# Other places in a block for a layer step's matmuls, its own-node product and two splits

## The reference

```python
x = _layernorm(x + _L0_gnn_ref(x, adj, W0, b0))     # D^-1/2 (A+I) D^-1/2 x W0^T + b0
x = _layernorm(x + _L1_gnn_ref(x, adj, WQ, WK, p))  # att[i,j] = p . relu(q[j] + k[i]), masked softmax over j, times x
x = _layernorm(x + _L2_gnn_ref(x, adj, W2, b2))     # as layer 0, with |A+I| in the degrees
x = _layernorm(x + _L3_gnn_ref(x, adj, W3, b3))     # without the identity added
```

## Time and profile before

| What | Value |
|---|---|
| median of 3 runs | 14251.69 us (14249.84 to 14259.41) |
| profiled execution, its own time | 14255.09 us |
| its span, first to last instruction | 14253.3 us |
| opening, to the first score matmul | 240.7 us |
| attention of the eight graphs | 240.7 to 14072.4 us |
| closing | 180.9 us |

### The profile page before, as it was taken

One profiled execution on the slowest core, in us unless ns is written; L12 is line 12 of the kernel. 1 busy time (PEld: TensorE's weight loads), 2 busy tenths in 40 slices (PEclk: granted clock), 3 DMA queues, 4 the chain that ended last, 5 costly groups with the idle time before them and its releaser, 6 DMA issues.

```text
span 14253.3 us, 317325 instructions
## 1 busy us (share of the span) xinstructions
PE 13023.6 (91%) x143877; PEld 5459.3 (38%) x143877; DVE 13509.2 (95%) x14168; ACT 13092.2 (92%) x8612; POOL 668.9 (5%) x495
## 2 busy tenths in 40 slices
PE   6889989999899988999989998899989999899988
PEld 3333334443344333443334433344333433333333
DVE  5999999999999999999999999999999999999995
ACT  5999899998999899998999989999899998998994
POOL 0000000000000000000000000000000000000000
PEclk7999999999999999999999999999999999999999
DMA  5111112221122111221122211222112221011103
GB/s 184 45 51 47 49 52 86 85 61 50 55 86 87 62 40 63 87 87 56 36 72 84 86 56 36 75 84 85 56 35 75 88 78 56 30 49 51 42 12 108
DMA packets 714328, 935.44 MB, mean 66 GB/s; under 512 B 61713, under 2 KB 455953, under 8 KB 693521
## 3 DMA queue, kind: packets, MB, share of 16 engines
q1 hardware_dynamic: 712976, 915.13, 20.5%
HBM read 722.01 MB, written 184.55 MB: 64 GB/s over the span
## 4 chain that ended last, share of the span: by engine, by line
PE 45%; DVE 35%; ACT 16%; issue 2%; DMA 2%; SPq 0%; POOL 0%; ACTq 0%; DVEq 0%; POOLq 0%
PE score L1134 33%; DVE big L990 31%; ACT big L756 14%; PE acc L1057 6%; PE turn L1034 2%; PE acc L1116 2%; DVE att L941 2%; DVE gx L871 1%; DMA piece<-adj_turned 1%; DMA big<-in_adj_dram 0%; ACT y_turned L679 0%; DVE stats L877 0%; ACT turned L669 0%; DMA q_pair_kept<-turned 0%; PE acc L1075 0%
## 5 line engine op out<-in xcount | busy, mean ns | idle before, releaser
L990 DVE TENSOR_SCALAR big<-q_pair,k_pair_cols 128x2048 f32<-128x2048 f32 x10240 | 12366.6, 1281 | 380.0 <-PE score L1134 362.6
L756 ACT ACTIVATE big<-q_f,k_cols 128x2048 f32<-128x2048 f32 x6144 | 11746.9, 1999 | 70.2 <-DMA q_f<-q_kept 44.1
L1134 PE MATMUL score<-big,unit_window 128*32 128x512 f16 x81920 | 5178.8, 396 | 819.0 <-DVE big L990 788.4
L1134 PE MATMUL score<-big,sign_window 128*32 128x512 f32 x49152 | 5619.7, 597 | 273.2 <-ACT big L756 268.6
L1134 PEld LDWEIGHTS score<-big,unit_window 128*32 128x32 bf16 x81920 | 2270.4, 96 | 4003.1 <-DVE big L990 1242.9
L1134 PEld LDWEIGHTS score<-big,sign_window 128*32 128x32 f32 x49152 | 1569.0, 110 | 3603.8 <-issue 3005.9
L1057 PE MATMUL acc<-piece,gs 128*128 128x512 f32 x3072 | 1446.6, 598 | 36.0 <-DMA piece<-adj_turned 23.6
L1057 PEld LDWEIGHTS acc<-piece,gs 128*128 128x128 f32 x3072 | 533.8, 191 | 545.4 <-issue 459.1
L737 ACT ACTIVATE att_turned<-turn 128x512 f32<-128x512 f32 x512 | 300.9, 588 | 390.5 <-PE turn L1034 389.7
L593 POOL TENSOR_SCALAR att_var<-att_mom 128x1 f32<-128x1 f32 x128 | 66.0, 515 | 10641.0 <-DVE att_mom L959 10641.0
L1116 PE MATMUL acc<-x,att_turned 128*128 128x128 f32 x4096 | 554.9, 279 | 0.0
(11 more groups left out here) (88 smaller groups left out, 2592.0 us busy)
## 6 DMA issues: line engine op xcount, KB each, us to landing
piece<-adj_turned SPq DMA_DIRECT2D x1536, 256.0 KB, 2.8
att<-in_adj_dram SPq DMA_DIRECT2D x128, 1024.0 KB, 5.1
raw<-in_adj_dram SPq DMA_DIRECT2D x224, 512.0 KB, 4.6
adj_turned<-turned SPq DMA_DIRECT2D x224, 512.0 KB, 4.3
big<-in_adj_dram SPq DMA_DIRECT2D x32, 512.0 KB, 7.6
adj_turned<-big SPq DMA_DIRECT2D x32, 512.0 KB, 6.9
gx<-in_x_dram SPq DMA_DIRECT2D x32, 256.0 KB, 4.2
q_kept<-raw SPq DMA_DIRECT2D x32, 256.0 KB, 3.4
```

The source lines that it names most:

```text
L756: ins = nc.scalar.activation(ring["A"][:, RANK[g] % RING * 4 + u, :], q_f32[:], ACT.Relu, bias=k_cols[:, t % 2, QUAD * u + g:QUAD * u + g ...
L990: ins = nc.vector.tensor_scalar(ring["D"][:, RANK[g] % RING * 4 + u, :], q_pair[:], k_pair_cols[:, t % 2, QUAD * u + g:QUAD * u + g + 1], ...
L1134: ins = nc.tensor.matmul(score[QUAD * u:QUAD * (u + 1), cc, :], window[:, QUAD - 1 - g:2 * QUAD - 1 - g], row, start=(g == 0 and part == 0 ...
```

## The change

Only tables of places change. No instruction is added or taken away. One piece moves from place 23 to place 0, and three from 23 to 18. The own-node product moves from 18 to 6. ScalarE's sum of the unit in slot 23 moves from place 25 to 23, ahead of A23. Its copy to `y_turned` moves from 26 to 25. The node scaling on VectorE and the q and k stages are given other places. The largest move among these is that of the split of k, from place 31 of the next block to place 5 of the block after it, with its high part and its store behind it.

```diff
-    SUM_UNIT = {0: 3, 6: 8, 10: 12, 14: 16, 18: 21, 23: 25, 28: 33}
+    SUM_UNIT = {0: 3, 6: 8, 10: 12, 14: 16, 18: 21, 23: 23, 28: 33}
-    PIECES_AT = {-4: [0, 1, 2], 0: [3, 4, 5], 6: [6, 7], 10: [8, 9], 14: [10], 18: [11], 23: [12, 13, 14, 15]}
-    SELF_AT, TURNED_AT, PROJECT_AT, SUM_AT, ROOT_AT, NORM_OUT_AT, STORE_AT = 18, 26, 28, 35, 36, 40, 41
-    SCALE_AT = {"layer2": [-25, -20, -15, -10], "layer3": [-5, -3, -1, 11], "layer0": [-5, -3, -1, 16]}
+    PIECES_AT = {-4: [0, 1, 2], 0: [3, 4, 5, 6], 6: [7, 8], 10: [9, 10], 14: [11], 18: [12, 13, 14, 15]}
+    SELF_AT, TURNED_AT, PROJECT_AT, SUM_AT, ROOT_AT, NORM_OUT_AT, STORE_AT = 6, 25, 28, 35, 36, 40, 41
+    SCALE_AT = {"layer2": [-25, -20, -15, -10], "layer3": [-5, -4, -3, 11], "layer0": [-5, -4, -3, 15]}
-    QK = {"turn": 46, "copy": 49, "q": 50, "q_out": 54, "k": 55, "q_store": 55, "q_split": 57, "k_out": 59,
-          "q_high": 60, "k_store": 60, "q_pair_store": 61, "k_split": 63, "k_high": 67, "k_pair_store": 69}
+    QK = {"turn": 46, "copy": 49, "q": 50, "q_out": 54, "k": 55, "q_store": 56, "q_split": 58, "k_out": 59,
+          "q_high": 61, "k_store": 61, "q_pair_store": 62, "k_split": 69, "k_high": 72, "k_pair_store": 73}
```

## The result

The changed kernel takes 14387.27 us (median of 4 runs, 14381.18 to 14398.32); the one before, beside it on the same chip, 14252.3. The ratio is 1.0095, with an interval of 1.0082 to 1.0108: slower by 135 us. The forecast was 14356. The measured median lies 2 us above the forecast's own range of 14330 to 14385, and inside the wider one, up to 14415, that takes in half of the clock's rival.

A forecast was written before the change was run, and what follows sets the result against it. No single engine but a loop of waits across TensorE, ScalarE and VectorE was taken as the bound. Six middle batches +92, first +4, last +13, opening -5 gave +104: median 14356 us, range 14330 to 14385.

The forecast's parts named there:

- the clock's rival: New waits before D25 and A23 bring TensorE's lower clock at D4 in eight layer blocks, seven batches: +83, 14440 us; chance 0.12.
- The bound, and the late D22: Three pieces more at place 18 put 2.58 us on TensorE before D19; D22 is late, layer 2 blocks grow 1.54 us.
- Two loops of waits: Loop of now, through A26, turns in 109.07 us; the one through D22 becomes longer, 110.61 us, after 1.00 us of slack.
- Its size in the undisturbed blocks: Growth per layer block: 1.5 us in 3 and 4, 2.3 in 5, 1.0 in 6 to 8, 1.8 in 9.
- The own-node product, "net nothing": Moved from place 18 to 6, +0.89 and -0.89 us on TensorE between D4 and D19, so no net cost.
- The sum of the unit, "hidden": Odd blocks: the sum delays A23 by some 2.5 us, TensorE waits 0.9; hidden because D27 starts late anyway, cover about 1 us.
- Layer 0: Blocks 10 to 13: late D22 costs 1.7, then 2.4 each, less the moved splits: +1.7, -0.7, -0.3, +1.3 us.
- The three gains of the splits: Split of k moved from ahead of D0 to place 5, ahead of D6: 3.1, 2.7 and 1.1 us gained in blocks 11 to 13.
- The rival in which the losses of clock go from these blocks: Blocks 11 to 13: TensorE's waits before D1 and D3 shrink, clock dips go, 31 less, opening 13 less: 14312 us; chance 0.15.
- Opening: The layer's sum goes ahead of the first split of k, which waits 8.15 us: between 0 and -18 us, taken as -5.
- Faster: Late D22 is made up, the loop through A26 is cut, blocks 2 to 9 gain 1.0 each: 14160 us; chance 0.06.
- no change: VectorE's share sets the time and its waits merely shift from D27 to D22: 14252 us, within 28; chance 0.06.

The follow-up runs named there:

- the fastest version: Kernel before with the new tables of q and k, three pieces at place 4 and one more moved from place 14 to 0: 14115.58 us, ratio 0.9903.

## Why the prediction was right, point by point

**The bound, and the late D22: right.** Two loops of waits lie near each other, and the change makes the second the longer. D22 waits 2.27 and 2.31 us in blocks 4 and 3 (2.2 foretold) and 2.31 in block 7 (2.3 foretold). The slack of 1.00 us at D27 and D1 is used up, TensorE waits at D25 where A23 did not wait first, and in the attention no split of k waits for a landing (in the opening four still do, up to 5.6 us). The two runs that move only the pieces put 151 and 128 us on this table.

**Its size in the undisturbed blocks: right, or a little high.** With the pieces alone, block 3 of c = 2 is 1.4 us longer (1.5 foretold). In the changed kernel block 4, with the clock kept, takes 110.24 us from D4 to D4 (110.6 foretold). Block 8 is 1.0 longer in the mean, as foretold, but 0.6 in the batches that keep the clock. Block 9 is 1.9 longer (1.8 foretold).

**The own-node product, "net nothing": wrong.** It costs 31 us by itself. The prediction counted the sum of TensorE's work between D4 and D19 and not its order. Work earlier in that stretch makes D9 and D11 late; work taken away behind them then meets a VectorE that is late too. The four parts alone come to 151 - 30 + 11 + 31 = 163 us, and together, with the two small tables that were not run alone, they give 135. That the product costs less in the changed kernel, since D19 is late there anyway, would fit this, but it was not put back there, so it is not shown.

**The sum of the unit, "hidden": wrong in blocks 3 and 7.** It costs some 11 us in the kernel before and 14 in the changed one, neither clear of the noise. The prediction had TensorE wait 0.9 us at A23 and the half tile come up to 1 us late in blocks 3 and 5, hidden as well. TensorE waits 1.4 to 1.5 us in block 5, 2.0 to 3.7 in block 3 and 2.3 to 3.4 in block 7. The half tile is late by up to 2.2 us, in blocks 3 and 7 and not in 5. In block 7 of all six batches and block 3 of three, A23 also loses its clock, after waits of 2.25 to 3.7 us. Then D24 is late for D27, which waits 1.0 to 2.9 us. In the three other batches of block 3, and in block 5, D27 does not wait, and the sum is hidden as foretold.

**The clock: in part the rival, not the forecast.** The forecast priced the middle batches at 92 us and they took 123.1. The excess of 31 us is 5.2 us a batch. It lies in blocks 3 (2.7), 7 (1.7), 10 (1.6) and 15 (0.9), with 1.7 in small amounts in other blocks and 3.5 the other way. In blocks 3, 7 and 15 rows show the slow matmuls: 1.67 us at D4 and A5, 1.70 at A23, 1.48 at D9. The rival expected one such loss at D4 in all eight layer blocks, 83 us. They come in some blocks and batches only: in the mean of the six batches D4 takes 2.85 and 2.93 us in blocks 3 and 6 (2.01 and 2.29 before), 2.12 and 2.00 in blocks 4 and 7. Block 10 has 3.37 (2.21 before). At D25, which the rival named too, the clock falls in every batch of blocks 9 and 10, after a wait of 2.15 us, and in no other layer block, after at most 1.7; block 9 is near its forecast all the same. Over the batch, the score groups spend 28.0 us beyond their 2.00 and 3.64 us each, 8.4 more than the 19.6 before. Not all of that is on the path, and in blocks 3 and 7 the late half tile has a share. So the clock, put at 0, is the term that was mis-sized most; the net excess of 31 us gives its size only roughly. The prediction took the kernel before as free of such losses in blocks 2 to 8. That holds for the batch c = 2 that it read; in other batches D4 of blocks 4 to 7 takes 2.8 to 3.5 us in some.

**Layer 0: near as a sum, wrong in its parts.** Foretold for blocks 10 to 13 was +2.0 us, measured +1.4; that these are close is luck. The three gains of the splits were put one block too early. The pieces alone cost 2.6 us in blocks 11 to 13 where 7.2 were foretold, as part of what came late was made up in the wait for the store and part in the clock. Gain and loss drew on the same wait, and the prediction counted it in both. The rival in which the losses of clock go from these blocks holds in part: D4 takes 2.00 us in block 11 of the changed kernel (3.13 before), but 3.51 and 3.49 in blocks 12 and 13, as before. With the tables alone it is block 13 that is freed, with the pieces alone blocks 12 and 13.

**Opening: under-sized**, -13.4 for -5, within the bounds of 0 and -18. The tables of q and k alone take 8.2 us off it, and the pieces alone 4.6, which the prediction did not name.

**Faster, and no change: shut out.** The late D22 is not made up, and the wait does not merely shift. But the part of the rival that sees a gain in the loop through A26 is real. With one piece less at 23 and D19 not late, the undisturbed block 3 is 108.8 for 109.1. It takes pieces put where TensorE waits to have it in full.

The Trainium skill, "Perfetto Trace Analysis", section "Optimization Strategy", says to take the gaps on the engine of highest occupancy and to ask what blocks there. This case agrees in the main: VectorE's wait for score matmuls is 362.6 us before, 538.7 after, 269.0 with three pieces at place 4 and 272.2 in the fastest version, at spans of 14253, 14383, 14141 and 14119. The last two show that this wait alone does not order them.

**Left open:** which blocks lose the clock. The same order of instructions with waits within a few hundredths of a microsecond keeps it in one batch and loses it in the next, so the runs give a size and a place for it and no rule. Why the place 0 piece, of all, brings it in nearly every block is not settled either.

## What to carry to other kernels

When engines with 91 to 95% run in fixed orders over small rings, find for each side job the next ring wait behind it and the slack that follows, and count the excess over that slack, once per period. Put independent matmuls right ahead of a group that TensorE regularly waits for: three of 0.86 us each in a wait of 2.8 us gave back 0.8% here. Look up when a load lands before its user is moved forward: here the same sum at 23 waited up to 0.6 us for its half tile with the pieces at place 23, and up to 2.2 us with them at 18. A job moved earlier on the same engine is not free because the sum up to the next wait is the same: each group between its two places must be looked at.

## What the runs showed that was not expected

A wait of 2.2 to 2.8 us on TensorE may or may not be followed by a stretch at the lower clock, with the same work before it: 2.00 against 3.48 us for D9 after waits of 2.24 and 2.29, 2.01 against 3.22 for D4 after 2.80 and 2.78, 3.64 against 5.34 for A26 after 2.06 in both. The D9 start 29.37 and 29.38 us after their block's first group, the D4 12.12 us in both. Each such loss costs 1.2 to 1.7 us in the groups that it meets. One at D4 makes the block 1.4 us longer, and two in block 15 make it 2.2 longer. Over the whole span the mean granted clock moved from 0.982 to 0.978 only:

```profile
core 0: 14383.2 us, clock 0.978
```

With the wait at D4 filled it is higher: 0.984 with three pieces at place 4 and with one more moved.
